# Row thresholds of a top-p attention: three guessed points for ScalarE's sums over two turns, a fourth score buffer, keys and adjacency in half the room

## The chip, the cores and the metric

The kernel runs on 1 of the 8 cores of a Trainium2 chip. The metric is the time of one execution on the device in microseconds, lower is better. PE is TensorE (matmuls and transposes), PEld its weight loads, DVE VectorE, ACT ScalarE, POOL GpSimd, SP the engine that issues the DMAs.

## The reference

Four graph layers on x (3327 x 256, padded to 26 tiles of 128 rows) with one adjacency matrix, each on relu(layernorm(x)) and added to x. The third one matters here:

```python
        logits = Q @ W2 @ K.T / TAU
        idx = jnp.argsort(-logits, axis=1)
        vals = jnp.take_along_axis(logits, idx, axis=1)
        csum = jnp.cumsum(jax.nn.softmax(vals, axis=1), axis=1)
        k_i = jnp.sum(csum < P_NUC, axis=1) + 1
        ...
        masked = jnp.where(keep, logits, -jnp.inf)
        return jax.nn.softmax(masked, axis=1)
    ...
    for s in range(STEPS):
        A = _adj_from_feats(Xa, W1, W2, W3)
        Xf = Rf @ Xf
        Xb = Rb @ Xb
        Xa = A @ Xa
        Z = Z + (Xf @ U1[s] + Xb @ U2[s] + Xa @ U3[s])
```

Q and K are Xa @ W1 and Xa @ W3, P_NUC is 0.9, STEPS is 2. So in each of two steps every row of 3327 scores needs its own threshold: the largest scores whose exponentials sum to 0.9 of the row are kept.

## The kernel before

The program is one `build()` with barriers between stages: the front (layer 0, sums of rows and columns), layer 1, the attention layer, layer 3. The change acts in the attention layer, which is software-pipelined over *turns*: `for i in range(rounds)` is unrolled on every engine, and tile t (0 to 25 are step 1, 26 to 51 step 2) passes through one stage a turn:

- turn t: `scores` on PE in four quarters k = 0 to 3 (two matmuls each on the halves of `K2` and `qt`), each quarter copied by ACT from `lg` to `E[:, t % 3]` (L1066). `neighbours` (L920) multiplies a quarter of an adjacency row block `adj` in each k, for the two linear branches.
- turn t + 1 (`exp_at`): DVE's row maximum (L1307), ACT's Exp with the sum Z (L1070) and six sums over the row, `fixed` (L1022): for each of three fixed points c the excess above c (Relu) and the count above c (Sign), two at each of k = 0, 1, 2. POOL's `bracket` (L1175 to L1219) then picks the two neighbouring points that enclose 0.9 Z.
- turn t + 2 (`search_at`): DVE's `find` (L1310). It waits for `bracketed`, makes EVALS = 3 passes in step 1 and 5 in step 2, each with `point` a trial threshold: L1345 sums the e above it, the small instructions around it (L1336 to L1349) move the ends and interpolate the next point. L1355 leaves in `U` what lies below the upper end. Then a loop takes the remaining values eight at a time in descending order (MAX8 L1368, MATCH_REPLACE L1378), one *round* or more until every one of the 128 rows has reached its share. L1394 writes the kept values back to E.
- turn t + 3 (`turn_at`): PE transposes E (L893), ACT copies to `PT` (L1062), PE multiplies with the values `Hc` (L880).
- turn t + 4 (`post_at`): scaling, dense products, and in step 2 two layer norms, whose scalars POOL computes (L1227 to L1235, L1258 to L1266).

PSUM holds one `lg` and one `tr`: a quarter's matmuls wait until ACT has copied the quarter before. ACT, DVE and POOL run their instructions in program order. In a turn ACT's order is, for each k, the PT copy, the score copy, at k = 0 the Exp and two sums, at k = 1 and 2 the copies of the dense products and two sums each, at k = 3 only copies. POOL's order is the second layer norm, the adds of Z and Y, the first layer norm, the adds of step 1, and last `bracket`. DVE's is the row maximum, then `find`.

SP loads each adjacency block in four chunks `adj[:, AGG[k]:AGG[k+1]]`; the chunk of the next block is issued as soon as `agg_part` says that this one has been used, a whole turn ahead. The stores of a turn stand behind its loads. Between the steps (`LAG` = 4 turns) nothing is scored, because step 2's keys are all of step 1's outputs; the linear branches start step 2 at `LATE` = 5.

Of the kernel before, what the change touches and what calls it, by code (L numbers as in the profile page):

```python
# [7 lines left out]
I32 = mybir.dt.int32  # L24
# [4 lines left out]
P = 128  # L29
# [4 lines left out]
EVALS = (3, 5)  # L34
MAX_AFTER = (1, 2)
AIM = 3.0
KEEP_END = 0.8

FIXED = (0.008, 0.03, 0.1)
NF = len(FIXED)  # L40
MARKED = -1.0
# [6 lines left out]
LAG = 4  # L48
LATE = 5
FIRST = 7  # L50
POINT, GAP, GOAL, MASS, BELOW = 0, 2, 3, 4, 5
# [27 lines left out]


def between_floats(value):


    t = np.float32(3 * value)
    while True:
        t = np.nextafter(t, np.float32(np.inf))
        near = [np.float32(t / np.float32(3))]
        for _ in range(2):
            near = [np.nextafter(near[0], np.float32(0))] + near + [np.nextafter(near[-1], np.float32(np.inf))]
        if all(np.float32(3) * e != t and 3 * float(e) != float(t) for e in near):  # L90
            return float(min(e for e in near if 3 * float(e) > float(t))), float(t)


def build(nc, n_nodes, xin, adjT, W0T, b0, W1g, A1T, A2, A3, UA, UB, UC, gamma, beta, tin, Wg3, out):
# [13 lines left out]
    with ctx:  # L108
# [43 lines left out]
        E = sb("E", [P, 3, NP])  # L152
# [6 lines left out]
        K2 = sb("K2", [P, NP])  # L159
# [93 lines left out]
        def layer(name, src_t, rhs, evac, dst_t, bufs):  # L253
# [6 lines left out]
            with phase_semaphores(nc, name + "_") as s:  # L260
# [11 lines left out]
                with nc.Block() as block:  # L272
# [106 lines left out]
                    def _(dve):  # L379
                        def body(u, par, live):  # L380
# [5 lines left out]
                            if live[2] and attention:  # L386
                                dve.wait_ge(dense_done, u - 1)
                                if later(u, 4):
                                    dve.wait_ge(q_out[par], 8 * (u - 2) + (0 if par == 0 else -8))
                                nc.vector.tensor_copy(K2[:, bass.ds((u - 2) * P, P)], dense[:, 0:P])  # L390
                                nc.vector.tensor_copy(qt[:, par], dense[:, P:2 * P]).then_inc(dense_copied, 1)
# [8 lines left out]
                        pipeline(dve, NT, body)  # L400

        xz = sb("xz", [P, 2, D])
# [250 lines left out]
        with ExitStack() as att:  # L653
            ab = lambda name, shape, dt=F32: att.enter_context(nc.sbuf_tensor(name, shape, dt))
            U = ab("U", [P, NPAD])
            PT = [ab(f"PT{k}", [P, 2, max(WIDE[k::2]) * P]) for k in range(2)]
# [3 lines left out]
            nmax = ab("nmax", [P, 2])  # L660
            Zs = ab("Zs", [P, 2])
            rz = ab("rz", [P, 4])
            over = ab("over", [P, 2, NF])
            sign = ab("sign", [P, 2, NF])
            neg_c = ab("neg_c", [P, NF])
            neg_3c = ab("neg_3c", [P, NF])
            half_c = ab("half_c", [P, NF])
            half_nc = ab("half_nc", [P, NF])
            table = ab("table", [P, NF + 2, 3])
            ft = ab("ft", [P, 2, NF])  # L670
            met = ab("met", [P, NF + 2])
            pick = ab("pick", [P, NF + 1])
            both = ab("both", [P, 2, NF + 1, 3])
            share = ab("share", [P, 5])
            ends2 = ab("ends2", [P, 2, 2, 3])
            trial2 = ab("trial2", [P, 2, 6])
            sp_ = ab("sp_", [P, 8])
            side = ab("side", [P, 2, 3], I32)
# [23 lines left out]
            side_at = lambda i: i - (NT + LAG + FIRST + 6) if 0 <= i - (NT + LAG + FIRST + 6) < NT // 2 else None  # L702
# [16 lines left out]
            rounds = NT + LAG + NT + 6  # L719
            early = NT - LAG  # L720
            spread = [b for i in range(rounds + 1) for b in [last_at(i)] if b is not None and i <= tiles + LATE]
# [5 lines left out]
            with phase_semaphores(nc, "att_") as s:  # L727
# [29 lines left out]
                search, rnd, fixed_done, consts = s("search_step"), s("round_step"), s("fixed_done"), s("consts")  # L757
                init, bracketed = s("bracket_step"), s("bracketed")

                with nc.Block() as block:  # L760
                    @block.sync
                    def _(sp):
                        def load_chunk(n, k):
                            j0, j1 = AGG[k], AGG[k + 1]
                            sp.dma_start(adj[:, j0:j1], adjT[n % NT, :, j0:j1]).then_inc(adj_in[k], 16)
# [5 lines left out]
                        for k in range(SLOTS):  # L771
                            load_chunk(0, k)
                        load_q(0)
                        load_q(1)
                        for i in range(rounds):
                            L, X, n = score_at(i), post_at(i), agg_at(i)
                            G = sent_at(i)
                            ahead = score_at(i + 1)
                            if ahead is not None and ahead >= 2 and ahead != NT and ahead != NT + 1:
                                sp.wait_ge(lg_done, SLOTS * (ahead - 1))  # L780
                                load_q(ahead)
                            if second(n):
                                b, q = n - NT, n % 2
                                if n >= NT + 2:
                                    sp.wait_ge(y1_done, b - 1)
                                sp.wait_ge(zg_out[b % 2], 16 * (b // 2 + 1))
                                sp.dma_start(zin[q][:, 0], zg_d[b]).then_inc(zin_in[q], 16)
                                sp.wait_ge(xo_out[b % 2], 16 * (b // 2 + 1))
                                sp.dma_start(zin[q][:, 1], xo_d[b, :, 0:D]).then_inc(zin_in[q], 16)
# [651 lines left out]
```

## Time and profile before

| | us |
|---|---|
| median of 3 runs (lowest, highest) | 3640.17 (3638.29, 3642.70) |
| span of the profiled execution | 3639.0 |
| PE busy | 3175.4 (87%) |
| DVE busy | 2635.1 (72%) |
| ACT busy | 1889.6 (52%) |
| POOL busy | 996.2 (27%) |
| PE weight loads | 2289.6 (63%) |

Busy time is the union of an engine's instructions. PE's is modelled at the ends of pipelined matmuls, so a busy PE is not a PE at its peak, and the reported lengths of POOL's instructions are rough. The first rows further down cut the attention layer at the starts of row maxima: 822 is tile 0's, 1763 tile 25's, 1871 tile 26's and 3266 tile 51's; the search of tile 51 ends at 3376, and layer 3 takes the rest. In all rows an instruction is named by its line in the kernel, its engine, its operation and `out<-in` by the program's names; a number in brackets behind an arrow is the idle time before it and what ended it.

### The profile page before, as it was taken

To read this page: it belongs to the slowest core of one execution; us is meant where nothing else is said; L and a number is where in the kernel's file an instruction comes from. 1 tells how busy PE (TensorE), PEld (TensorE's weight loads), DVE (VectorE), ACT (ScalarE), POOL (GpSimd) and SP (SyncE) were. 2 spreads that over 40 slices of the span, in tenths; PEclk is the share of its full clock that TensorE was granted. 3 is DMA by queue.
4 is the path that set the end of the run, shared out by engine and by line. 5 is a ranking of instruction groups with operands and counts; after the bars stand their busy time and mean duration, and the time that the engine had idled before them with its cause. 6 is when DMAs were issued, how large, how long until landed. Compare 5 with 4: busy or idle time off the path is not lost. (4 is left out here: it accounts for less than half of the span.)

```text
span 3639.0 us, 40362 instructions
## 1 busy us (share of the span) xinstructions
PE 3175.4 (87%) x13212; PEld 2289.6 (63%) x13212; DVE 2635.1 (72%) x3794; ACT 1889.6 (52%) x2355; POOL 996.2 (27%) x2293
## 2 busy tenths in 40 slices
PE   4999899987999999999875878667899889996799
PEld 3788688875677776777633445344555555554688
DVE  6963400006999999999839999999999999998100
ACT  2211311218788787888744556545565556563100
POOL 1212411211122221212211334334434334334211
PEclk9999999988999999999987989888999999998899
DMA  6544444432122221212221111111122222222255
GB/s 251 209 156 137 129 154 162 160 119 64 51 67 61 55 69 56 67 56 56 58 82 39 51 48 44 45 40 49 51 80 63 68 78 58 76 81 75 69 196 179
DMA packets 142416, 328.49 MB, mean 90 GB/s; under 512 B 15457, under 2 KB 95393, under 8 KB 130977
## 3 DMA queue, kind: packets, MB, share of 16 engines
q1 hardware_dynamic: 142240, 326.31, 28.3%
q8 instruction: 90, 1.47, 0.2%
q14 instruction: 86, 0.70, 0.1%
HBM read 287.59 MB, written 38.67 MB: 90 GB/s over the span
## 5 line engine op out<-in xcount | busy, mean ns | idle before, releaser
L1345 DVE SCALAR_TENSOR_TENSOR U<-E,trial 128x3327 f32<-128x3327 f32 x208 | 778.0, 3740 | 0.0
L880 PE MATMUL bank<-Hc,PT 128*128 128x256 f32 x2704 | 647.0, 392 | 68.8 <-ACT PT L1062 68.8
L880 PEld LDWEIGHTS bank<-Hc,PT 128*128 128x128 f32 x2704 | 528.0, 197 | 194.4 <-ACT PT L1062 92.3
L920 PE MATMUL bank<-big,adj 128*128 128x512 f32 x1352 | 613.7, 605 | 0.0
L1022 ACT ACTIVATE junk<-E,neg_3c 128x3327 uint8<-128x3327 f32 x156 | 479.1, 3071 | 5.1
L1022 ACT ACTIVATE junk<-E,neg_c 128x3327 uint8<-128x3327 f32 x156 | 479.6, 3074 | 1.7
L920 PEld LDWEIGHTS bank<-big,adj 128*128 128x128 f32 x1352 | 254.9, 194 | 329.4 <-issue 327.6
L893 PE MATMUL tr<-ident,E 128*128 128x128 f32 x1352 | 200.3, 291 | 275.5 <-DVE E L1394 275.5
L1062 ACT ACTIVATE PT<-tr 128x1024 f32<-128x1024 f32 x208 | 176.9, 851 | 369.2 <-PE tr L893 369.2
L893 PEld LDWEIGHTS tr<-ident,E 128*128 128x128 f32 x1352 | 172.8, 151 | 305.9 <-DVE E L1394 287.4
L920 PE MATMUL bank<-Hc,adj 128*128 128x256 f32 x1352 | 319.1, 388 | 0.0
L1368 DVE MAX8 top<-U 128x8 f32<-128x3327 f32 x81 | 293.8, 3627 | 24.5 <-DVE U L1378 12.4
L920 PEld LDWEIGHTS bank<-Hc,adj 128*128 128x128 f32 x1352 | 257.3, 194 | 82.1 <-issue 50.7
L1378 DVE MATCH_REPLACE8 U<-mark,U 128x3336 f32<-128x3336 f32 x81 | 293.1, 3618 | 0.0
L1307 DVE TENSOR_REDUCE nmax<-E 128x1 f32<-128x3327 f32 x52 | 187.8, 3611 | 109.5 <-ACT E L1066 73.8
L313 PE MATMUL bank<-big,adj 128*128 128x256 f32 x1170 | 263.6, 386 | 4.0 <-PEq L64 3.8
L313 PE MATMUL bank<-big,E 128*128 128x256 f32 x1170 | 256.8, 379 | 0.0
L313 PEld LDWEIGHTS bank<-big,adj 128*128 128x128 f32 x1170 | 224.2, 193 | 39.4 <-issue 8.8
L908 PE MATMUL lg<-K,qt 64*128 64x384 f32 (+1 forms) x832 | 223.1, 615 | 23.0 <-ACT E L1066 12.7
L313 PEld LDWEIGHTS bank<-big,E 128*128 128x128 f32 x1170 | 221.2, 190 | 29.8 <-DMA E<-adjT 0.2
L385 DVE TENSOR_TENSOR t<-bank,big 128x256 f32<-128x256 f32 x26 | 11.0, 425 | 288.3 <-PE bank L313 288.3
L1066 ACT ACTIVATE E<-lg 128x1024 f32<-128x1024 f32 x208 | 178.1, 856 | 55.1 <-PE lg L908 53.4
(231 smaller groups left out, 4481.7 us busy)
## 6 DMA issues: line engine op xcount, KB each, us to landing
adj<-adjT SPq DMA_DIRECT2D x131, 448.0 KB, 3.4
E<-adjT SPq DMA_DIRECT2D x32, 1664.0 KB, 7.0
adj<-adjT SPq DMA_DIRECT2D x104, 384.0 KB, 3.4
adj<-adjT SPq DMA_DIRECT2D x20, 1664.0 KB, 7.0
adj<-adjT SPq DMA_DIRECT2D x14, 1216.0 KB, 5.7
E<-adjT SPq DMA_DIRECT2D x13, 1216.0 KB, 5.8
xt<-xin SPq DMA_DIRECT2D x52, 128.0 KB, 5.8
x_d<-xn SPq DMA_DIRECT2D x52, 128.0 KB, 1.7
```

Source lines behind the costliest of these rows:

```text
L313: last = nc.tensor.matmul(acc[par][:, 0:D], bufs[par][:, j], rhs[:, j], start=(j == j0), stop=(j == NT - 1))
L880: last = mm(axp[:, 0:D], PT[k % 2][:, h, i * P:(i + 1) * P], Hc[:, j], start=(k == 0 and h == 0 and i == 0), stop=(k == SLOTS - 1 and h == ...
L893: last = nc.tensor.transpose(tr[:, h, i * P:(i + 1) * P], E[:, t % 3, c0:c0 + P], ident[:])
L908: last = mm(lg[:, h, 0:w], qt[rows, t % 2], K2[rows, c0:c0 + w], start=True, stop=True)
L920: last = mm(agg[:, 0:w], adj[:, j], rhs[:, j], start=(j == 0), stop=False)
L1022: go(junk[:, 0:N], E[:, t % 3, 0:N], func, bias=less[:, c:c + 1], scale=scale, accum_out=acc_[:, t % 2, c:c + 1]).then_inc(fixed_done, 1)
L1062: go(PT[k % 2][:, :, 0:w], tr[:, :, 0:w], ACT.Copy).then_inc(pt_copied, 1)
L1066: go(halves(E[:, L % 3])[:, :, c0:c0 + w], lg[:, :, 0:w], ACT.Copy).then_inc(lg_copied, 1)
L1307: V_.tensor_reduce(nmax[:, t % 2:t % 2 + 1], E[:, t % 3, 0:N], axis=AX_X, op=ALU.max, negate=True).then_inc(max_ready, 1)
L1345: V_.scalar_tensor_tensor(out=U[:, 0:N], in0=e, scalar=point, in1=e, op0=ALU.is_ge, op1=ALU.mult, accum_out=found))
L1368: rthen(V_.memset(U[:, N:NPAD], 0.0), V_.max(top8[:], U[:, 0:N]))
L1378: V_.match_replace(U[:], mark[:], U[:], MARKED).then_inc(rnd, 1)
```

## The change

- The three fixed points become three guessed ones per row. POOL's `guess(t)` computes the first from the row's mean (which the score copies now accumulate in `musum`), its maximum and Z, as if scores were normally distributed; `update(t, j)` takes ACT's sums at point j, tightens the ends and computes the next point by a Newton step with a corrected slope. ACT makes two sums at points 0 and 1 and one at point 2 (`PASSES`), five instead of six, and each now waits (`aimed[j]`) until POOL has offered the point.
- These are spread over two turns: guess, sums at point 0 and update 0 in turn t + 1; sums at points 1 and 2, updates 1 and 2 in turn t + 2 (`aim_at`); the search moves to t + 3, the transposes to t + 4, the rest to t + 5. `E` has four buffers (`DEPTH`), LAG is 5 and LATE 7, and there are two more turns in all.
- DVE's EVALS falls from (3, 5) to (2, 3). The last pass over E accumulates what it leaves, and the mass above is Z less that.
- To make room: `K2` holds keys in half the columns (each half of the partitions its own half of the keys), `adj` is used in 14 blocks and not 26, in two places of 7 (`SPAN`), so that chunk k + 2 is issued when chunk k has been used; `xz` and one `PT` lie in the rest of `adj`. SP's order in a turn changes: the stores of the last turn come behind the first chunk.
- DVE's part of layer 1 is unrolled.

```diff
-EVALS = (3, 5)
+EVALS = (2, 3)
+PASSES = (2, 2, 1)
-LAG = 4
-LATE = 5
+DEPTH = 4
+LAG = 5
+LATE = 7
+SPAN = 7
...
-            search_at = lambda i: shown(i - 2)
-            turn_at = lambda i: shown(i - 3)
-            post_at = lambda i: shown(i - 4)
+            aim_at = lambda i: shown(i - 2)
+            search_at = lambda i: shown(i - 3)
+            turn_at = lambda i: shown(i - 4)
+            post_at = lambda i: shown(i - 5)
...
+                        def sums(t, j, m):
+                            if m == 0:
+                                act.wait_ge(aimed[j], t + 1)
+                                if j > 0:
+                                    act.wait_ge(summed[j - 1], PASSES[j - 1] * (t + 1))
+                                elif t >= 1:
+                                    act.wait_ge(summed[2], t)
+                            else:
+                                act.wait_ge(summed[j], 2 * t + 1)
+                            func, acc_ = ((ACT.Relu, over), (ACT.Sign, sign))[m if j < 2 else 1]
+                            go(junk[:, 0:N], E[:, t % DEPTH, 0:N], func, bias=negp[:, t % 2, j:j + 1], scale=1.0,
+                               accum_out=acc_[:, t % 2, j:j + 1]).then_inc(summed[j], 1)
...
-                                    fixed(F, 0, 2)
+                                if k == 0 and R is not None:
+                                    sums(R, 1, 0)
+                                if k == 3 and F is not None:
+                                    sums(F, 0, 1)
-                                    if F is not None:
-                                        fixed(F, 2, 4)
+                                    if R is not None:
+                                        sums(R, 1, 1)
+                                    if R is not None:
+                                        sums(R, 2, 0)
                                     if F is not None:
-                                        fixed(F, 4, 2 * NF)
+                                        sums(F, 0, 0)
...
+                        def offer(t, j):
+                            then(ts(negp[:, t % 2, j:j + 1], cand[:, t % 2, 0:1], -UNDER, None, ALU.mult))
+                            pool.sem_inc(aimed[j], 1)
...
+                            pool.wait_ge(exp_done, t + 1)
+                            if t >= DEPTH:
+                                pool.wait_ge(probs_ready, t - DEPTH + 1)
+                            then(tt(ga[:, q, 0:2], musum[:, q, 0:2], musum[:, q, 2:4], ALU.add),
+                                 tt(ga_(2), z, root, ALU.pow))
+                            then(tt(ga_(3), ga_(0), ga_(1), ALU.add),
+                                 ts(ga_(4), ga_(2), ROOT, -ROOT - math.log(N), ALU.mult, ALU.add))
+                            then(ts(ga_(5), ga_(3), 1.0 / N, nm, ALU.mult, ALU.add))
+                            then(tt(ga_(6), ga_(4), ga_(5), ALU.subtract))
...
+                            if j > 0:
+                                then(tt(up_(16), mass_, up_(7 + j), ALU.subtract))
+                                then(ts(up_(17), up_(16), up_(16), up_(3), ALU.mult, ALU.add),
+                                     tt(up_(18), up_(16), up_(20), ALU.mult))
+                                then(tt(up_(19), up_(17), minus, ALU.pow),
+                                     tt(up_(18), up_(4), up_(18), ALU.subtract))
+                                then(tt(slope, up_(18), up_(19), ALU.mult))
...
+                                guess(F)
...
+                                update(R, 1)
...
+                                update(R, 2)
+                            if F is not None:
+                                update(F, 0)
...
-                                                         op0=ALU.is_ge, op1=ALU.subtract, reverse1=True))
+                                                         op0=ALU.is_lt, op1=ALU.mult, accum_out=sc[:, 5:6]))
+                            then(V_.tensor_tensor(mass[:, 0:1], Zs[:, q:q + 1], sc[:, 5:6], ALU.subtract))
```

`then(...)` gives each of its instructions a semaphore increment and waits for all of them before the next call. In order, with (n) instructions: guess() has the groups 2, 2, 1, 1, 2, 2, 1, 1, 1, then the offer 1, then 4, 3 and the three of `prepare`; update 0 has 14 instructions besides its `prepare`, update 1 has 21, update 2 has 22 and no `prepare`. POOL's order in a turn is: adds of Z (step 2), adds of Y, one small one, guess(F), one small one, update(R, 1), the rest of both layer norms, adds of step 1, update(R, 2), update(F, 0), and last the two adds that end step 2's tile.

## Rows read from the trace of the kernel before

**Rows 1.** By stretch: us; busy PE, PEld, DVE, ACT, POOL (instructions); PE clock; DMA share; GB/s.

```profile
822.00:1763.00 941.00, 894.20 (x4098) 668.17 (x4097) 845.66 (x1197) 779.60 (x758) 212.57 (x605) 0.97 0.21 60
1763.00:1871.00 108.00, 74.57 (x332) 55.08 (x330) 64.24 (x96) 44.84 (x55) 14.34 (x46) 0.86 0.17 52
1871.00:3266.00 1395.00, 1164.48 (x4000) 682.32 (x4001) 1299.31 (x1994) 814.60 (x899) 492.54 (x927) 0.92 0.20 59
3266.00:3376.00 110.00, 65.28 (x253) 45.25 (x252) 97.27 (x155) 39.12 (x55) 44.35 (x81) 0.84 0.26 85
```

**Rows 2.** The same view, two turns, then twelve turns of step 2.

```profile
1461.00:1498.00 37.00, 37.00 (x176) 28.08 (x175) 33.72 (x49) 31.59 (x31) 9.41 (x26) 1.00 0.22 62
2122.00:2178.00 56.00, 45.93 (x154) 26.20 (x154) 53.88 (x84) 33.35 (x38) 21.48 (x40) 0.90 0.17 49
...
2603.00:3266.00 663.00, 608.43 (x2184) 373.44 (x2183) 624.59 (x965) 404.38 (x468) 252.42 (x482) 0.96 0.24 70
```

**Rows 3.** Waits: engine and line, who it waited for, us in total, times, longest.

```profile
PE tr L893 <- DVE E L1394: 275.5, 28, 37.0
...
DVE sc L1343 <- POOLq L1218: 73.1, 29, 5.7
```

**Rows 4.** Timeline of DVE, a tile of step 1, step 2's first maximum: start, us, instruction.

```profile
1197.16 3.61 DVE L1307 TENSOR_REDUCE nmax<-E 128x1 f32<-128x3327 f32 x1
...
1200.88 3.67 DVE L1345 SCALAR_TENSOR_TENSOR U<-E,trial 128x3327 f32<-128x3327 f32 x1
...
1206.15 3.68 DVE L1345 SCALAR_TENSOR_TENSOR U<-E,trial 128x3327 f32<-128x3327 f32 x1
...
1215.71 3.68 DVE L1355 SCALAR_TENSOR_TENSOR U<-E,ends 128x3327 f32<-128x3327 f32 x1
...
1219.63 3.63 DVE L1368 MAX8 top<-U 128x8 f32<-128x3327 f32 x1 [0.24 <-DVE U L1355]
...
1228.46 3.60 DVE L1394 SCALAR_TENSOR_TENSOR E<-U,E 128x3327 f32<-128x3327 f32 x1
...
1871.28 3.62 DVE L1307 TENSOR_REDUCE nmax<-E 128x1 f32<-128x3327 f32 x1 [35.70 <-issue]
```

**Rows 5.** Timeline of DVE and POOL around one bracket, step 1.

```profile
1531.50 3.62 DVE L1394 SCALAR_TENSOR_TENSOR E<-U,E 128x3327 f32<-128x3327 f32 x1
...
1531.61 3.56 POOL L1194 TENSOR_TENSOR trial<-Zs,share 128x1 f32<-128x1 f32 x1
...
1535.96 0.19 POOL L1199 TENSOR_TENSOR trial<-trial,share 128x1 f32<-128x1 f32 x1
1536.12 0.31 POOL L1200 TENSOR_SCALAR met<-table,trial 128x3 f32<-128x3 f32 x1
1536.51 0.47 POOL L1202 TENSOR_TENSOR met<-met 128x1 f32<-128x1 f32 x2
...
1539.06 0.57 POOL L1214 TENSOR_TENSOR sp_<-sp_,share 128x1 f32<-128x1 f32 x1
1539.60 0.19 POOL L1215 TENSOR_TENSOR sp_<-sp_,ends 128x1 f32<-128x1 f32 x1
1539.87 0.20 POOL L1216 TENSOR_TENSOR sp_<-sp_ 128x1 f32<-128x1 f32 x1
```

**Rows 6.** One line of POOL (second layer norm): min/median/max ns.

```profile
L1235 POOL TENSOR_TENSOR stat<-stat x26: 191/3396/3405, 2085.2 to 3410.4; 128x1 f32<-128x1 f32 x26
```

**Rows 7.** Timeline of ACT in step 1: two sums and a fourth score copy.

```profile
1471.10 3.07 ACT L1022 ACTIVATE junk<-E,neg_c 128x3327 uint8<-128x3327 f32 x1
...
1474.30 3.07 ACT L1022 ACTIVATE junk<-E,neg_3c 128x3327 uint8<-128x3327 f32 x1
...
1495.28 0.80 ACT L1066 ACTIVATE E<-lg 128x768 f32<-128x768 f32 x1
```

**Rows 8.** DMA issues: tile, count, KB each, us to landing.

```profile
adj<-adjT SPq DMA_DIRECT2D x131, 448.0 KB, 3.4
```

**Rows 9.** Groups of DVE's instructions, stretch of step 2.

```profile
L1368 DVE MAX8 top<-U 128x8 f32<-128x3327 f32 x51 | 185.0, 3627 | 16.9 <-DVE U L1378 10.8 <-DVE U L1355 5.8 <-issue 0.3
```

More of the change, by code:

```diff
@@ L78, in pipeline @@
         static(u)
[L81 to L91, printed above, removed]
 def build(nc, n_nodes, xin, adjT, W0T, b0, W1g, A1T, A2, A3, UA, UB, UC, gamma, beta, tin, Wg3, out):
@@ L659, in build @@
             stat3 = ab("stat3", [P, 2, 8])
-            nmax = ab("nmax", [P, 2])
-            Zs = ab("Zs", [P, 2])
+            nmax = ab("nmax", [P, DEPTH])
+            Zs = ab("Zs", [P, DEPTH])
             rz = ab("rz", [P, 4])
[L663 to L678, printed above, removed]
+            musum = ab("musum", [P, 2, SLOTS])
+            over = ab("over", [P, 2, 2])
+            sign = ab("sign", [P, 2, POINTS])
+            negp = ab("negp", [P, 2, POINTS])
+            known = ab("known", [P, 8])
+            outset = ab("outset", [P, 2, 2, 2])
+            ga = ab("ga", [P, 2, 20])
+            up = ab("up", [P, 2, 24])
+            cand = ab("cand", [P, 2, 3])
+            took = ab("took", [P, 3])
+            parts = ab("parts", [P, 2, 2, 2])
+            ends2 = ab("ends2", [P, DEPTH, 2, 2])
+            trial2 = ab("trial2", [P, DEPTH, 5])
+            side = ab("side", [P, 2, 2], I32)
             sc = ab("sc", [P, 8])
@@ L718, in build @@
             last_at = lambda i: post_at(i - 2) - NT if second(post_at(i - 2)) else None
-            rounds = NT + LAG + NT + 6
+            rounds = NT + LAG + NT + 7
             early = NT - LAG
-            spread = [b for i in range(rounds + 1) for b in [last_at(i)] if b is not None and i <= tiles + LATE]
+            spread = [b for i in range(rounds + 1) for b in [last_at(i)] if b is not None and i < tiles + LATE]
             kept = len(spread)
@@ L919, in neighbours @@
                             for j in range(AGG[k], AGG[k + 1]):
-                                last = mm(agg[:, 0:w], adj[:, j], rhs[:, j], start=(j == 0), stop=False)
+                                last = mm(agg[:, 0:w], adj[:, SPAN * (k % 2) + j - AGG[k]], rhs[:, j], start=(j == 0), stop=False)
                             if k == SLOTS - 1:
@@ new lines, in _, with then, restart @@
+                        pool.wait_ge(step_done, len(values))
+                        pool.sem_clear(step_done)
+                        root, minus, half, e_ = (known[:, i:i + 1] for i in range(4))
+                        n = [0]
+                        def then(*ins):
+                            for i in ins:
+                                i.then_inc(step_done, 1)
+                            n[0] += len(ins)
+                            pool.wait_ge(step_done, n[0])
+                        def restart():
+                            pool.sem_clear(step_done)
+                            n[0] = 0
@@ L1267, in _ @@
+                            if R is not None:
+                                update(R, 2)
+                            if F is not None:
+                                update(F, 0)
+                            if second(X):
+                                b, q = X - NT, X % 2
                                 pool.wait_ge(c_ready, b + 1)
```

427 lines of the change are left out of this document (229 added, 198 removed).

## The prediction, made before the changed kernel was run

> **What bounds the kernel now.** I read the busy times by stretch first, then two short stretches inside the attention stage, then the waits, then single turns in order of time. The busy shares of the whole span say little. Cut at the first and last row maximum of each attention step [rows 1], the span falls into step 1 (941 us, tiles 0 to 25), a drain between the steps (108), step 2 (1395, tiles 26 to 51) and the last search (110); layer 3 and the front stay as they are. One turn of step 1 takes 37 us and PE is busy in all of it, while DVE has 33.7 and ACT 31.6 [rows 2] (first line). In step 2 a turn takes 56, DVE is busy 53.9 of it and PE 45.9 [rows 2] (second line). PE's longest wait is for DVE's final E, 275.5 us in 28 waits, and DVE waits 73 us for POOL's bracket [rows 3]. So step 1 is bound by PE except where a tile needs a second extraction round, step 2 by DVE. POOL is never late today: it works 213 us in step 1 and 493 in step 2 [rows 1].
>
> **What the change takes from DVE and ACT.** One pass over E with its small steps is 1206.15 - 1200.88 = 5.27 us [rows 4]. EVALS goes from (3, 5) to (2, 3): 26 x 1 + 26 x 2 = 78 passes, 411 us off DVE. A turn of DVE in step 1 falls from 33.7 to 28.4, one of step 2 by 10.5: the 53.9 are a tile with two rounds of MAX8 and MATCH_REPLACE, a round is 8.8 from 1219.63 to 1228.46 [rows 4] and 8.2 of it busy, so with one round 45.7 now and 35.2 then. ACT makes 5 sums a tile and not 6, 3.2 us each [rows 7]: 166 us off it, less 0.2 x 4 x 52 = 42 for the new row sums of the copies. The accumulated marking pass is the same pass of 3.68 us with one small step more. Moved to a turn of their own, sums and bracket are ready before DVE asks, so its 73 us of waiting go as well. If nothing else were late next, PE would be.
>
> **What it adds to POOL.** Counted from the diff, a tile now has, instead of bracket()'s 23 instructions, 87: 45 TENSOR_SCALAR, 33 TENSOR_TENSOR, 9 powers, nearly all in a chain in which each waits for the one before. Prices from POOL's bracket [rows 5]: a dependent step costs its duration and 0.08, so 0.27 for a TENSOR_TENSOR (1539.60 to 1539.87), 0.39 for a TENSOR_SCALAR (1536.12 to 1536.51), 0.65 for a power (0.57 + 0.08); all but the last of a group cost 0.16 (1535.96 to 1536.12), 0.27 and 0.54 (1539.06 to 1539.60). That gives 5.3 us for guess() up to its offer and 8.4 in all, 4.5 and 5.5 for update 0, 6.8 and 7.8 for update 1, 7.0 for update 2: 28.7 us a tile, where the bracket took 5.5. The durations alone (45 x 0.31 + 33 x 0.19 + 9 x 0.57) would be 25.3; the Trainium skill (Perfetto Trace Analysis, GPSIMD Instruction) says to time POOL by the spacing of starts and not by reported spans, which is what the steps above do; by the spans a turn would be about 3 us shorter. The TENSOR_SCALARs of the change have two operations where the one in the trace has one: bounds 0.27 (a TENSOR_TENSOR's price) and 0.51 (0.39 and 0.12 again). I take 0.39, the row of the same instruction.
>
> **What holds POOL.** A POOL instruction of 0.19 us took 3.56 at 1531.61, and ended with the pass that DVE had begun at 1531.50 [rows 5]; L1235, 128x1, has a median of 3.40 over 26, against a minimum of 0.19 [rows 6]. The first began while L1394 ran, the others while L1345 did: DVE's long passes with two inputs, E and E or U and E. While a row maximum runs, from 1535, the same kind takes 0.19 [rows 5]. So POOL stands still during each SCALAR_TENSOR_TENSOR over 3327 columns. There are 4 such passes a tile in step 1 after the change (two trials, mark, final; 14.7 us) and 5 in step 2 (18.4). The Trainium skill (SBUF — State Buffer, Who interferes with whom) has this as a lock: a DVE instruction with two SBUF inputs and a GpSimd instruction that reads SBUF exclude each other, and a reduction never takes part. It speaks against this change, the trace agrees (3.40 and 3.56 against 0.19), and where it would have the earlier one delay the other too, that falls on DVE, which gets slack.
>
> **The turn, walked through.** ACT executes in order, and its sums now wait for POOL: sums(R, 2, 0) and sums(F, 0, 0) stand at k = 2, ahead of the fourth PT copy and the fourth score copy, which let DVE's next maximum start. A sum is 3.2 us (1471.10 to 1474.30), the copy 0.8 (1495.28) [rows 7]; today no sum waits. POOL in the new turn, from the fourth copy: it waits for the last sum (3.2), then update 0 (5.5), guess (8.4), update 1 to its offer (6.8); then ACT: two sums (6.4) and two copies with the read (1.7). 32.0 us of chain. With POOL free it fits inside PE's 36.9. DVE's next maximum begins with that copy, and its passes fall at 3.7 to 7.4, 9.0 to 12.7, 13.3 to 17.0 and 26.0 to 29.6 after it ([rows 4], with one pass of 5.27 taken out). POOL has work in each of them: update 0 from 3.2 to 19.8, guess to 31.8, the offer at 38.6, sums to 45.0, copies to 46.7. 32.0 + 14.7 = 46.7 us a turn, against 941 / 25 = 37.6 now. In step 2 POOL also has the two layer norms, three adds of Z, two of Y and two at the end: some 6.0 us of it in the chain (0.8 a 256-wide one). 38.0 + 18.4 = 56.4 us, against 1395 / 25 = 55.8 now; DVE with one to three rounds (35 to 52) and PE (608 of 663 us over 12 turns, 50.7 each, third line of [rows 2]) hide in that.
>
> **The rest.** The keys in half the room: the same matmuls, and copies of half the partitions. The adjacency blocks have half a turn of lead instead of one, some 18 us for a transfer of 3.4 [rows 8]; if that cover went, a chunk would cost up to 3.4 us, four times a turn. SP issues the stores of the last turn behind the first chunk of this one: SP waits there for POOL's x3 and ACT's copies, and behind it stand the chunks for k = 3 and the next turn; they have two quarters of slack, so nothing. LAG and the fourth buffer add one turn to each drain. Between the steps, from tile 25's maximum: tile 24's update 2 ends at 49 and its search runs to 75; update 0 of tile 25 falls between its passes (offer at 65), two sums 71, update 1 behind the final pass 82, sum 85, update 2 at 92, search of 26 us to 118. Now that search ends 108 less DVE's wait of 35.7 [rows 4] after the maximum, at 72: +46. At the end, with the norms on POOL and a pass more, tile 51's update 2 comes near 114 and its search ends at 150, against 110 [rows 1]: +40. In exchange the first turns of either step, without searches, run at 20 and 35 us.
>
> **Sum,** on the profiled execution's 3639 (the median is 3640.2, 1 above; I add it): step 1: 22 + 35 + 23 x 46.7 = 1131 against 941, +190. Drain +46. Step 2: 20 + 35 + 2 x 52.8 + 55.9 + 20 x 56.4 = 1344 against 1395, -50. End +40. 3639 + 226 + 1 = 3866. Each us of chain is worth 46 us of time.
>
> **Rivals.** (a) POOL's steps are cheaper: TENSOR_SCALAR at 0.27 takes 33 x 0.12 = 4.0 us off the chain, -184; and an instruction that is already reading when a pass starts goes on beside it, some 0.2 x 4 a turn, -37: 3645, with a spread to either side of no change. Chance 0.17. (b) The other side: POOL isn't in the way, because the passes fall where it waits for ACT anyway. It decides at 36.9 - 32.0 = 4.9 us of blocked time a turn, little over one pass of the four. Then PE sets both steps: 22 + 30 + 23 x 36.9 = 901 (-40), drain +10, step 2: 20 + 30 + 10 x 45.9 + 13 x 50.7 = 1168 (-227), end +8: 3391 with the 1 above. For it: POOL works only 493 of 1395 us now [rows 1], and a turn apart there is room; against it: each of its chains is longer than DVE's gaps of 1.6 us. Chance 0.15 for anything from 3390 to 3570. (c) The change doesn't do what it says: three guesses and two or three passes leave rows further off than a bracket and three or five, and rounds multiply. Step 2 has 51 for its 26 tiles today [rows 9]. DVE passes 56.4 only from (56.4 - 35.2) / 8.2 + 1 = 3.6 rounds a tile; 4.5 would be +190: 4050. Chance 0.07. (d) TENSOR_SCALAR at 0.51: +4.0, +184: 4050; part of the forecast's upper end.
>
> **Chances.** The forecast 0.61, (a) 0.17, (b) 0.15, (c) 0.07. Range 3540 to 4010: it takes in (a), the part of (b) in which a pass or two still lie in the way, and the forecast with a TENSOR_SCALAR up to 0.47; it leaves most of (b), (c) and (d)'s end. A measurement here can tell 0.2%, 7 us. Faster: (b) and under half of (a), 0.22; same 0.04; slower 0.74.
>
> **What would show it.** In the changed kernel: POOL busy near 80% or more of the attention stage, with median durations near 3 us in a share of its 128x1 instructions; ACT's largest waits for POOL's negp; PE idle some 10 us a turn in step 1; DVE waiting for E's fourth copy, not for POOL; turns of 46.7 and 56.4 that no longer follow the number of rounds. Turns of 37 in step 1, and PE waiting for nothing, would show (b); MAX8 well over 81, (c); waits of PE on adj, the halved room.

## The result and the profile after

The changed kernel takes 3737.1 us (median of 4 executions, 3736.5 to 3738.1) against 3640.9 for the kernel before, measured beside it: 1.026 times as long, interval 1.025 to 1.028, so +96 us where +226 was forecast. The profiled execution's span is 3736.2 us, with VectorE (DVE) busy 58% of it, PE 87% and GpSimd (POOL) 64%.

By the starts of row maxima, as for the kernel before, the span falls into:

| stretch | before | forecast | after | difference | forecast difference |
|---|---|---|---|---|---|
| to tile 0's maximum | 821.8 | | 817.0 | -5 | 0 |
| step 1 (25 turns) | 941.5 | 1131 | 1081.7 | +140 | +190 |
| drain between the steps | 107.9 | 154 | 150.9 | +43 | +46 |
| step 2 (25 turns) | 1394.6 | 1344 | 1273.1 | -122 | -50 |
| tile 51's search | 109.8 | 150 | 149.5 | +40 | +40 |
| the rest | 263.3 | | 264.1 | +1 | 0 |

The same stretches, the third line of them step 2, then one turn of each step (columns as in [rows 1]: length, busy PE, PEld, DVE, ACT, POOL with instructions, PE clock, DMA share, GB/s):

```profile
817.00:1898.00 1081.00, 925.94 (x4009) 679.86 (x4008) 693.04 (x886) 692.39 (x790) 884.45 (x2154) 0.92 0.18 52
1898.00:2049.00 151.00, 98.99 (x420) 74.31 (x419) 79.00 (x109) 60.89 (x77) 68.37 (x161) 0.82 0.12 36
2049.00:3322.00 1273.00, 1122.47 (x3841) 659.88 (x3842) 960.41 (x1338) 715.96 (x918) 1079.49 (x2457) 0.94 0.21 62
3322.00:3472.00 150.00, 110.99 (x410) 74.39 (x408) 107.38 (x156) 58.13 (x86) 112.63 (x217) 0.89 0.28 87
1046.70:1091.70 45.00, 38.59 (x174) 28.57 (x173) 28.66 (x37) 28.78 (x34) 37.18 (x90) 0.96 0.19 52
2750.00:2803.70 53.70, 51.47 (x192) 31.23 (x189) 34.65 (x50) 30.23 (x41) 46.33 (x105) 1.00 0.26 72
```

Against [rows 1], DVE's load in step 1 fell from 846 to 693 us and in step 2 from 1299 to 960, as the removed passes should make it; POOL's rose from 213 to 884 and from 493 to 1079. POOL is busy 82 to 85% of both steps and the short gaps between its dependent instructions fill nearly all the rest. The largest waits say the same (engine and line, whom it waited for, us in total, times, longest):

```profile
DVE nmax L1375 <- ACT E L1070: 690.2, 46, 36.4
...
ACT junk L1027 <- POOLq L1197: 329.0, 54, 17.6
...
PE bank L882 <- ACT PT L1066: 278.2, 75, 9.5
...
POOL up L1253 <- ACT junk L1027: 61.0, 50, 6.2
PE tr L895 <- DVE E L1460: 50.3, 4, 22.4
...
DVE sc L1411 <- POOLq L1288: 75.9, 8, 20.7
```

DVE waits for the fourth score copy, ACT's sums (L1027) wait for POOL's offer of a point (L1196, L1197), PE waits for ACT's copies to `PT` that stand behind those sums; the wait of PE for DVE's final E, 275.5 in [rows 3], has shrunk to 50.3. At the head of update 0 POOL waits for ACT only 61 us in 50 turns. DVE's wait for POOL, 73 us before [rows 3], is 75.9 now, but in another place: four waits of 15 to 21 us in the two drains make up 70.7 of it, the turns only 5. It is the chain of the forecast.

One turn of step 1, from maximum to maximum: DVE's long instructions, then those of POOL that open a part of its walk or are long, then ACT's (start, us, instruction):

```profile
1046.69 3.62 DVE L1375 TENSOR_REDUCE nmax<-E 128x1 f32<-128x3327 f32 x1 [15.41 <-ACT E L1070]
1050.42 3.68 DVE L1413 SCALAR_TENSOR_TENSOR U<-E,trial 128x3327 f32<-128x3327 f32 x1
1055.69 3.68 DVE L1413 SCALAR_TENSOR_TENSOR U<-E,trial 128x3327 f32<-128x3327 f32 x1
1059.89 3.68 DVE L1420 SCALAR_TENSOR_TENSOR U<-E,ends 128x3327 f32<-128x3327 f32 x1
...
1068.79 3.62 DVE L1444 MATCH_REPLACE8 U<-mark,U 128x3336 f32<-128x3336 f32 x1
...
1072.69 3.61 DVE L1460 SCALAR_TENSOR_TENSOR E<-U,E 128x3327 f32<-128x3327 f32 x1
1091.72 3.62 DVE L1375 TENSOR_REDUCE nmax<-E 128x1 f32<-128x3327 f32 x1 [15.42 <-ACT E L1070]
```

```profile
1049.72 0.19 POOL L1253 TENSOR_SCALAR up<-sign 128x1 f32<-128x1 f32 x1 [1.31 <-ACT junk L1027]
...
1050.46 3.81 POOL L1261 TENSOR_SCALAR cand<-up 128x2 f32<-128x2 f32 x1
...
1055.64 0.57 POOL L1277 TENSOR_TENSOR up<-known,up 128x1 f32<-128x1 f32 x1
1056.19 3.24 POOL L1278 TENSOR_TENSOR ends<-parts 128x4 f32<-128x4 f32 x1
...
1059.82 3.79 POOL L1283 TENSOR_SCALAR cand<-up,ends 128x1 f32<-128x1 f32 x1
...
1065.37 0.19 POOL L1216 TENSOR_TENSOR ga<-musum 128x2 f32<-128x2 f32 x1 [0.24 <-POOL up L1204]
...
1069.36 0.55 POOL L1228 TENSOR_TENSOR cand<-known,ga 128x1 f32<-128x1 f32 x1
...
1071.03 0.57 POOL L1234 TENSOR_TENSOR ga<-Zs,known 128x1 f32<-128x1 f32 x1
...
1072.65 3.78 POOL L1202 TENSOR_SCALAR up<-known,cand,ga 128x2 f32<-128x2 f32 x1
...
1077.26 0.19 POOL L1253 TENSOR_SCALAR up<-sign 128x1 f32<-128x1 f32 x1 [0.19 <-POOL up L1204]
...
1083.42 0.21 POOL L1196 TENSOR_SCALAR negp<-cand 128x1 f32<-128x1 f32 x1
```

```profile
1083.72 3.07 ACT L1027 ACTIVATE junk<-E,negp 128x3327 uint8<-128x3327 f32 x1 [5.37 <-POOLq L1197]
1086.97 3.07 ACT L1027 ACTIVATE junk<-E,negp 128x3327 uint8<-128x3327 f32 x1
1090.04 0.79 ACT L1066 ACTIVATE PT<-tr 128x768 f32<-128x768 f32 x1
1090.73 0.80 ACT L1070 ACTIVATE E<-lg 128x768 f32<-128x768 f32 x1
```

Read it as the forecast walked it. POOL waits for the last sum until 1049.72 (L1253 opens update 0), the guess begins at 1065.37 (L1216), update 1 at 1077.26, its offer at 1083.42 starts ACT's two sums at 1083.72, the two copies follow, and the next maximum stands at 1091.72: 45.03 us. Four POOL instructions of 3.2 to 3.8 us lie in it, each ending within 0.2 us of the end of one of the four two-input passes.

### The profile page after: what moved, and what is told of

The parts are those of the page before. It is cut to its first block and busy times, and to the rows that moved or that the text cites. A ratio compares the mean times of both kernels' runs of the same rounds, so it can differ in the third digit from the quotient of the medians.

```text
span 3736.2 us, 43278 instructions
## 1 busy us (share of the span) xinstructions
PE 3234.8 (87%) x13212; PEld 2326.9 (62%) x13212; DVE 2169.4 (58%) x2838; ACT 1739.3 (47%) x2461; POOL 2374.9 (64%) x5618
## 5 line engine op out<-in xcount | busy, mean ns | idle before, releaser
L1027 ACT ACTIVATE junk<-E,negp 128x3327 uint8<-128x3327 f32 x260 | 797.6, 3068 | 548.9 <-POOLq L1197 329.0
L882 PE MATMUL bank<-Hc,PT 128*128 128x256 f32 x1248 | 392.6, 479 | 278.2 <-ACT PT L1066 278.2
L882 PEld LDWEIGHTS bank<-Hc,PT 128*128 128x128 f32 x1248 | 297.3, 244 | 378.5 <-ACT PT L1066 321.8
L1413 DVE SCALAR_TENSOR_TENSOR U<-E,trial 128x3327 f32<-128x3327 f32 x130 | 479.3, 3687 | 0.0
L922 PEld LDWEIGHTS bank<-big,adj 128*128 128x128 f32 x1352 | 250.9, 190 | 319.9 <-issue 318.9
L294 PE MATMUL bank<-big,E 128*128 128x256 f32 x1664 | 365.6, 381 | 4.1 <-DMA E<-adjT 2.1
L882 PE MATMUL bank<-Hc,adj 128*128 128x256 f32 x1456 | 340.2, 386 | 13.8 <-ACT adj L1066 13.8
L882 PEld LDWEIGHTS bank<-Hc,adj 128*128 128x128 f32 x1456 | 281.4, 194 | 77.4 <-issue 23.4
L922 PE MATMUL bank<-Hc,adj 128*128 128x256 f32 x1352 | 317.9, 387 | 5.5 <-ACT bias L1047 5.4
L922 PEld LDWEIGHTS bank<-Hc,adj 128*128 128x128 f32 x1352 | 256.6, 193 | 85.3 <-issue 54.0
L895 PE MATMUL tr<-ident,E 128*128 128x128 f32 x1352 | 187.9, 279 | 50.4 <-DVE E L1460 50.3
L1261 POOL TENSOR_SCALAR cand<-up 128x2 f32<-128x2 f32 x156 | 201.1, 1289 | 15.6
L1420 DVE SCALAR_TENSOR_TENSOR U<-E,ends 128x3327 f32<-128x3327 f32 x52 | 201.7, 3878 | 2.2
```

The source lines that it names most:

```text
L294: last = nc.tensor.matmul(acc[par][:, 0:D], bufs[par][:, j], rhs[:, j], start=(j == j0), stop=(j == NT - 1))
L882: last = mm(axp[:, 0:D], PT[k % 2][:, h, i * P:(i + 1) * P], Hc[:, j], start=(k == 0 and h == 0 and i == 0), stop=(k == SLOTS - 1 and h == ...
L895: last = nc.tensor.transpose(tr[:, h, i * P:(i + 1) * P], E[:, t % DEPTH, c0:c0 + P], ident[:])
L922: last = mm(agg[:, 0:w], adj[:, SPAN * (k % 2) + j - AGG[k]], rhs[:, j], start=(j == 0), stop=False)
L1027: go(junk[:, 0:N], E[:, t % DEPTH, 0:N], func, bias=negp[:, t % 2, j:j + 1], scale=1.0, accum_out=acc_[:, t % 2, j:j + 1]).then_inc(summed ...
L1261: then(ts(cand[:, q, 1:3], up[:, q, 0:2], mass_, None, ALU.add), ts(took[:, 1:2], reach, tgt, None, ALU.is_ge))
```

## Experiments

In order of what they tell, not of when they ran. Each was timed over 4 executions; the kernel before, run beside them, had medians of 3640.5 to 3641.2. The rounds named are executions of MAX8 (81 before, 75 in the changed kernel: 29 in step 1, 46 in step 2). The length of a turn is the median of the 25 turns of its step, unless one turn is named.

**One more pass of DVE a tile, with two inputs or with one.** Ahead of the trial loop a pass over E whose sum nobody uses:

```diff
                             dve.wait_ge(bracketed, t + 1)
+                            # e1
+                            then(V_.scalar_tensor_tensor(out=U[:, 0:N], in0=e, scalar=point, in1=e,
+                                                         op0=ALU.is_ge, op1=ALU.mult, accum_out=sc[:, 7:8]))
+                            # e2, in its place
+                            then(V_.tensor_reduce(sc[:, 7:8], e, axis=AX_X, op=ALU.max))
```

> The changed kernel with one more pass in each search, of the kind of its trials: two inputs, E and E, 3.68 us, into U, which the next pass overwrites. The result does not change. VectorE is idle some 16 us of a turn of 45 in step 1. Theory (POOL's chain sets the turn, and every two-input pass holds it up): a turn of step 1 goes from 45.0 to 48.7, one of step 2 from 53.8 to 57.5, the drains by 10 to 15 in all: about +185, 3920 us. Rival (the turn is the chain through POOL and ACT alone, VectorE has slack): turns stay at 45.0 and 53.8, +15 from the drains: 3750.

> The changed kernel with one more pass in each search as well, but a reduction with one input (3.6 us, a maximum over E into an unused scalar). Theory (the lock between two-input passes and POOL): turns stay at 45.0 and 53.8, only the drains grow: +10 to +20, 3750 us. Rival (it is VectorE's time as such that counts, whatever the pass reads): as the two-input pass, +170 to +190.

Measured: 3908.7 us with the two-input pass (+172 against the changed kernel; turns of 48.2 and 57.4 instead of 45.0 and 53.7), 3736.4 with the one-input pass (no change; turns 44.8 and 53.6, those of step 2 now spread from 47 to 62, step 2 as a whole again 1273). Both passes keep DVE busy for about as long (3.68 and 3.61 us). The added reduction of the second kernel runs from 1140.97 to 1144.58, and POOL works through it at full pace, twelve instructions begun; with the next two-input pass, begun at 1144.81, it stops. That kernel, DVE then POOL:

```profile
1140.97 3.61 DVE L1401 TENSOR_REDUCE sc<-E 128x1 f32<-128x3327 f32 x1
1144.81 3.68 DVE L1414 SCALAR_TENSOR_TENSOR U<-E,trial 128x3327 f32<-128x3327 f32 x1
```

```profile
1141.20 0.31 POOL L1261 TENSOR_SCALAR cand<-up 128x2 f32<-128x2 f32 x1
...
1143.68 0.19 POOL L1279 TENSOR_TENSOR up<-up,cand 128x1 f32<-128x1 f32 x1
...
1144.87 3.84 POOL L1202 TENSOR_SCALAR up<-known,cand,ga 128x2 f32<-128x2 f32 x1 [0.22 <-POOL negp L1196]
```

So it is not DVE's time that costs, it is what a two-input pass does to POOL. The two added passes differ in one more thing: the first also writes all its columns to `U`, the second a single one. The changed kernel's trace settles that. MATCH_REPLACE8 reads and writes 3336 columns, with a single input of that width, and POOL runs beside it at its usual pace (1068.79 in the turn above, with the powers of 1069.36 and 1071.03 at 0.55 and 0.57 us). In the 75 rounds no POOL instruction begun beside MAX8 or MATCH_REPLACE8 took over 0.74 us.

**One pass of trial less a tile.** `EVALS = (2, 3)` becomes `(1, 2)`.

> The changed kernel with one pass of trial less in each tile (1 and 2 in place of 2 and 3), so that more is left to the rounds of MAX8 and MATCH_REPLACE8. Theory: a pass that reads two inputs holds GpSimd for its whole length while a round does not, and GpSimd's walk bounds the turn: each turn is shorter by 3.2 to 3.7 us (45.0 to 41.6 and 53.7 to 50.2), whatever the rounds do, as long as VectorE does not become the bound; over 51 turns 3560 to 3590 us. Rival: the rounds that come in its place (7.2 us each on VectorE, perhaps 20 to 40 of them) land on the path: 3737 or more.

Measured: 3603.3 us (ratio to before 0.990, interval 0.988 to 0.991). Turns of 41.9 and 50.6, each 3.1 us shorter, while the rounds rose from 75 to 119:

```profile
L1434 DVE MAX8 top<-U 128x8 f32<-128x3327 f32 x119 | 431.6, 3627 | 41.8 <-DVE U L1444 29.5 <-DVE mass L1422 12.3
```

44 rounds more, some 8 us of DVE each, and 134 us less time: the turn follows POOL and not DVE. It falls 13 us outside what was expected; the drain grew by 7 us, and some tiles of step 1 with four rounds took turns of 51 us.

**Ten more instructions on POOL**, at the head of update 0, each waiting for the one before:

```diff
+                            if j == 0:
+                                for _ in range(10):   # e8
+                                    then(ts(padded[:], known[:, 0:1], 1.0, 0.0, ALU.mult, ALU.add))
+                            # e9, in its place: ts(padded[:], known[:, 0:1], known[:, 1:2], known[:, 2:3], ...)
                             then(ts(count, sign[:, q, j:j + 1], 0.5, N / 2, ALU.mult, ALU.add))
```

> The changed kernel with ten more TENSOR_SCALAR on GpSimd in a row, each waiting for the one before, at the head of update 0, with two constants and no scalar read from memory (their results are used nowhere). Theory: GpSimd's walk round the turn is the bound, so each of some 48 turns grows by ten steps. At the 0.27 us that the changed kernel's trace shows for such a step: +2.7 us a turn, 3860 to 3875 us. At the 0.39 us that the prediction took: +3.9 us a turn, 3920 to 3930 us. If GpSimd is not the bound of a turn: below 3780 us.

> As the run with ten more TENSOR_SCALAR on GpSimd, but each of the ten reads its two scalars from memory instead of having them as constants. The run with constants grew by 146 us, 2.8 us a turn. Theory: the price of this operation depends on how many scalars it reads; the changed kernel's trace shows 0.43 us a step for two of them, so +4.3 us a turn over 51 turns: 3737 + 220 = 3957 us, some 73 above the run with constants. If the scalars cost nothing and the difference in the trace has another reason: 3883 us again.

Measured: 3883.2 us with constants (turns 47.8 and 56.5, +2.8 each), 3979.5 with scalars from memory (49.5 and 58.6, +4.5 and +4.9). The added instructions in either kernel (min/median/max ns; the maxima are held by passes):

```profile
L1256 POOL TENSOR_SCALAR padded<-known x520: 190/191/3692, 840.7 to 3534.1; 128x1 f32<-128x1 f32 x174
```

```profile
L1256 POOL TENSOR_SCALAR padded<-known x520: 343/345/3887, 841.1 to 3634.5; 128x1 f32<-128x1 f32 x174
```

A dependent TENSOR_SCALAR costs 0.28 us with two constants and 0.45 with two scalars read from memory; [rows 5]' 0.39 for an instruction with one such scalar was taken for all 45. The second kernel came out 22 us above what was expected, the first 8 to 23. Both show that the walk of POOL is the turn, at about one us of turn for one us of walk, in both steps.

**ACT's sums of the new point before the last sum of the old one.** At k = 2 the order is turned (the semaphore waits in `sums()`, which are not shown, are fitted to it):

```diff
-                                    if R is not None:
-                                        sums(R, 2, 0)
                                     if F is not None:
                                         sums(F, 0, 0)
+                                    if R is not None:
+                                        sums(R, 2, 0)
```

> The changed kernel with ScalarE's sums(F, 0, 0) ahead of sums(R, 2, 0) at k = 2: it then fills the 6 us in which ScalarE waits for update 1. Theory A (the ring through both engines sets the turn: update 0, guess, update 1, two sums, two copies, a sum): 3.2 us off the ring, turns of 41.8 and 50.6, -147: 3590 us. Theory B (POOL's own work with the passes that hold it, 43.5 of the 45.0, is the next bound at once): 1.5 a turn, -65: 3670.

Measured: 3717.7 us, -19. Both expectations were too large. The turn of step 1 fell by 1.1 us (45.0 to 43.9), that of step 2 by 0.2. POOL sat idle 1.3 us a turn of step 1 before update 0 ([1.31 <-ACT junk L1027] in the timeline above), and 0.36 in the turn of step 2 shown further down. Nearly all of that is gone now (25.9 us in 9 waits in place of 61.0 in 50), and it was all there was: with POOL at work in the whole turn, moving ACT's sums can't shorten it. The mechanism is theory B's, at 1.1 us where it had 1.5, and in step 1 only. Theory A counted the sum as part of a chain, although POOL has another update to do meanwhile.

**Two guessed points instead of three, in both steps.** `PASSES = (2, 2)`, no update 2.

> The changed kernel with two guessed points and not three: no sums(R, 2, 0), no update 2, update 1 gives the search's first point. POOL loses 22 instructions and 7 us a turn, ScalarE a sum. Theory (POOL sets the turn): a turn of step 1 falls from 45.0 to PE's 37, one of step 2 from 53.8 to 47 to 50, if rounds stay near 29 and 46: about 3440 us. Rival (fewer points cost as much in rounds as they save): rounds above 2 a tile in step 1 and 2.7 in step 2, where VectorE takes over: 3600 to 3750.

Measured: 3752.9 us. POOL's walk is shorter by 27 instructions a turn, and step 1 still grew, from 1082 to 1171: its rounds went from 29 to 79, and DVE is busy 1067 of 1171 us. Step 2 shrank, from 1273 to 1208, with 59 rounds in place of 46, and the last search from 150 to 129. So the third point earns its time in step 1 and not in step 2, although there the rounds already come unevenly: one tile needs nine, and one turn takes 105.5 us.

**The guess taken back.** The frame of the change stays (fourth buffer, one turn more, half room); in step 1 or in both steps the fixed points, six sums and `bracket` of the kernel before come back (cut; in e5 two constants of the interpolation in step 2, `AIM` and `KEEP_END`, also get their values of before):

```diff
-EVALS = (2, 3)
+EVALS = (3, 5)                  # e5; (3, 3) in e6 and e7
+FIXED_STEP = (True, True)       # e5; (True, False) in e6 and e7
+LAST = (2, 2)                   # last guessed point; (2, 1) in e7
...
-                            if F is not None:
-                                guess(F)
+                            if isg(F):
+                                guess(F)
...
+                            if isf(F):
+                                bracket(F)
```

> The changed kernel with the guess taken back in both steps: three fixed points, six sums and the bracket of the kernel before, with 3 and 5 rounds of trial; the fourth score buffer, the longer order of turns and the half room stay. If all of the loss of step 1 is the chain of guess and update, step 1 takes 940 us again (turns 36.9), the drain between the steps about 120, and step 2 loses the wait for the bracket that the kernel before had (73 us in all): about 1330; in all 3570 to 3640 us. If the loss came from the fourth buffer or the longer order, the turns of step 1 stay at 42 us or more: 3730 or more.

> Step 1 with the three fixed points and its 3 rounds, step 2 with the three guessed points and its 3 rounds. If the two steps are bounded apart from each other, step 1 and the drain take about 150 + 25 us less than in the changed kernel and step 2 stays at 1273: 3540 to 3580 us, below the kernel before by 2 to 3%. If the guess's load in step 2 depended on the points of step 1 (it doesn't by the chain), 3650 or more.

> As the run with fixed points in step 1, but step 2 takes two guessed points instead of three. The run with two points in both steps had a step 2 of 1208 us and a last search of 129 us: so 3450 to 3500 us if the steps are independent; 3560 or more if the third point is what keeps step 2's rounds down.

Measured: 3600.4, 3554.0 and 3468.7 us. With the guess out of both steps the frame alone is worth 40 us: step 1 takes 914 and step 2 1325, and DVE's wait for the bracket, 73 us in [rows 3], is no longer among the forty largest. Which part of the frame gives how much of the 40, no run separates. Set against this kernel, the guess with its fewer passes costs 168 us in step 1 (1082 for 914) and gains 52 in step 2 (1273 for 1325): of the 122 us that step 2 gained in the change, the frame alone has 69. Fixed points in step 1 and three guessed ones in step 2 give 914 and 1273, the two halves of the other kernels put together. With two guessed points in step 2 the kernel is 4.7% faster than the kernel before (ratio 0.953, interval 0.951 to 0.954). Its step 1, drain, step 2 and last search:

```profile
818.60:1732.00 913.40, 873.61 (x3998) 650.01 (x3997) 819.91 (x1173) 783.13 (x850) 249.99 (x603) 0.98 0.22 62
1732.00:1867.00 135.00, 95.67 (x432) 72.57 (x431) 95.38 (x146) 51.92 (x70) 25.60 (x48) 0.88 0.14 41
1867.00:3075.00 1208.00, 1074.34 (x3810) 630.61 (x3811) 1073.18 (x1470) 652.50 (x872) 898.00 (x1820) 0.94 0.22 64
3075.00:3204.00 129.00, 113.41 (x441) 75.90 (x439) 114.64 (x167) 52.33 (x81) 96.63 (x151) 0.97 0.34 106
```

PE is busy 874 of 913 us in step 1, and in the last turns of step 2 nearly all the time:

```profile
2680.00:3075.00 395.00, 391.68 (x1457) 242.14 (x1456) 339.74 (x470) 224.75 (x313) 317.88 (x616) 1.00 0.27 79
```

**The same with a pass less in step 2**, `EVALS = (3, 2)`:

> The kernel with fixed points in step 1 and two guessed points in step 2, with 2 passes of trial in step 2 in place of 3. Theory: with two points GpSimd's walk is no longer what bounds step 2 (the turns take 48.7 us, TensorE's own work in a turn some 45), and the rounds are already 59; a pass less saves 3.7 us a tile on VectorE and costs 20 or more rounds of 7.2: 3450 to 3500 us, about the same as with 3 passes (3469). If the lock of the pass still bounds the turns: 3400 or less.

Measured: 3677.5 us, a miss, 209 above the kernel with three passes. The rounds of step 2 went from 59 to 104 and the median turn only from 48.7 to 49.3, but seven tiles had five rounds or more (one before), one of them eleven, and there are turns of up to 120 us. I had counted rounds as a mean that DVE's slack could hide; they come in lumps. (Rounds of the whole attention layer:)

```profile
L1536 DVE MAX8 top<-U 128x8 f32<-128x3327 f32 x134 | 486.0, 3627 | 43.6 <-DVE U L1546 32.0 <-DVE mass L1524 11.5
```

## Why the prediction was right or wrong

**What the change takes from DVE and ACT** was right: over the whole execution DVE has 466 us less to do (411 were charged for the removed passes, and six rounds fewer are some 50 more) and ACT 150 (124 forecast), and PE hardly waits for DVE any more. The 153 and 339 us by which DVE's load fell in the two steps overstate it a little, because with the later search a part of it has moved to the drains.

**What holds POOL** was right as a mechanism, shown by the pair of added passes, and a little too dear. Each pass was charged its whole 3.68 us. In the turn above the four held instructions cost 3.81, 3.24, 3.79 and 3.78 in place of the 0.30, 0.20, 0.33 and 0.34 that they take undisturbed: 13.45 in all, 3.4 a pass, against 14.7. It is no single turn's number: over the last 22 turns of step 1 four instructions a turn were held, for 13.5 us beyond their shortest time, and over the last 21 of step 2 five, for 16.6. The rows before the change had this already: 3.56 less 0.19 is 3.37 [rows 5], and the median of 3.40 less 0.19 is 3.2 [rows 6]. The prediction read these lines as a halt during each pass and then charged the pass's own 3.68. What POOL has begun when a pass starts is finished first: the L1278 held for 3.24 waited behind a power of 0.57 (L1277) that had begun 0.05 before the pass of 1055.69. A pass added costs 3.2 and 3.7 us a turn, one removed saves 3.1. The Trainium skill (SBUF — State Buffer, Who interferes with whom) has the pair locked for a whole instruction and lets the order of issue decide who waits; the rows agree where POOL came second, with its instructions at 3.2 to 3.8 us. Where POOL came first they agree only in part: the power of 1055.64 left the pass of 1055.69 at 3.68 us (more in the last section).

**The chain of a turn** was right in all its links. Measured on the turn above, with the held time taken out, against the forecast: wait for the last sum 3.0 (3.2), update 0 with its offer and the preparation 5.6 (5.5), guess 8.5 (8.4), update 1 to its offer 6.5 (6.8), two sums 6.3 (6.4), copies 1.7 (1.7). 31.6 against 32.0. The price of 0.39 for every TENSOR_SCALAR was wrong one by one (0.28 to 0.45), but the instructions of the chain have zero, one and two scalars from memory in such a mix that POOL's three links come to 20.6 against 20.7. That is luck and not a right price. The bounds of 0.27 and 0.51 held. One thing the walk didn't compare: POOL's own work in the turn, with the passes that hold it, is only 1.3 us shorter than the turn, so that the wait for the last sum is a link nearly without weight (ACT's sums turned round gave 1.1).

**The step that failed: two terms of the sum were mis-sized, the turn and the first turns.** The turn was forecast 1.7 us too long in step 1 (46.7 against 45.0) and 2.7 in step 2 (56.4 against 53.7). Of the first, 1.3 is the price of a pass, charged at 3.68 and measured at 3.4, and 0.4 the links, as above. In the step 2 turn from 2750 to 2803.7, five POOL instructions were held:

```profile
2750.26 3.99 POOL L1361 TENSOR_TENSOR kq<-xo,cc 128x256 f32<-128x256 f32 x1
...
2763.35 3.50 POOL L1231 TENSOR_TENSOR parts<-Zs,outset 128x4 f32<-128x4 f32 x1 [0.18 <-POOL negp L1196]
...
2788.45 3.82 POOL L1261 TENSOR_SCALAR cand<-up 128x2 f32<-128x2 f32 x1
2794.19 3.24 POOL L1278 TENSOR_TENSOR ends<-parts 128x4 f32<-128x4 f32 x1
2799.13 3.69 POOL L1203 TENSOR_SCALAR up<-cand 128x1 f32<-128x1 f32 x1
2803.18 0.72 POOL L1354 TENSOR_TENSOR cc<-cc,gam 128x256 f32<-128x256 f32 x1
```

Their excess over 0.73, 0.20, 0.30, 0.20 and 0.26 is 16.5 us (18.4 charged), and the rest of the turn 37.2 (38.0). The error of a turn is multiplied by some 46 turns, as the prediction itself said: the last 22 turns of step 1 are 40 us less than forecast, the last 21 of step 2 55. The first turns of either step came 25 us shorter in all. In step 1 they were put at 22, 35 and 46.7 and came at 19.9, 30.8 and 44.1; in step 2 at 20, 35, 52.8 and 52.8, and came at 15.7, 30.8, 53.5 and 44.7. The first two of either step, which have no search and so no passes, are 15 of the 25; the prediction gives no working for them. With 3 from the drain and 4 from the stretches outside, that is all but 2 of the 129 between 3866 and 3737. The error is 4 to 5% of each turn. But the gain and the loss of the change nearly cancel, and so this error of 129 us is more than the whole measured difference of 96.

**Drain and end**, walked link by link, came out at +43 and +40 against +46 and +40. Between the steps the links are there one by one: the searches of tiles 24 and 25 began 47 and 88.5 us after tile 25's maximum (49 and 92 forecast), and the last one ended at 115 (118). That the end fits to the us is luck: tile 51's update 2 was done 106 us after its maximum, where some 114 was forecast, and its search, with two rounds, took 44 us and not 36.

**Rivals.** (a) had a cheaper TENSOR_SCALAR and 0.2 us off each pass, and put the time at 3645: its two reasons are both there in part, its size isn't (1.7 and 2.7 us off a turn, where it had 4.8). (b), POOL not in the way, fell in both steps: ten instructions more lengthen the turn by their whole length, where PE as the bound would hide them. Its point of decision (4.9 us of blocked time a turn) was passed with 13.5. (c), rounds multiplying, did not happen with three points (75 for 81), but did with two in step 1 (79 for 29) and with a pass less (119 for 75).

**Signs.** POOL at 82 and 85% of the two steps, ACT waiting for the offers, DVE for the fourth copy, and turns that don't follow the rounds (tiles of step 2 with one to three rounds all take 53.4 to 54.0) came as written. PE's idle was forecast at 10 us a turn and is 6.4 of 45.0.

## What to carry to other kernels

Before small scalar work goes to GpSimd, lay its chain beside VectorE's passes: each long pass with two inputs stops it for nearly that pass, while a reduction, MAX8 or MATCH_REPLACE8 doesn't, so a pass saved on VectorE can be worth more to GpSimd than to VectorE. Ask of each stage alone whether a moved computation pays: here the same guess, against the frame without it, lost 168 us in the step bound by TensorE and won 52 in the one bound by VectorE, and splitting it by stage turned a kernel 2.6% slower into one 2.4% faster (3554.0 us), and 4.7% with one point less in step 2. Where a forecast is one turn's length multiplied by some fifty turns, take what each stop costs from the rows that show it (the held length less the undisturbed one), and not from the length of the instruction that causes it: two us a turn were here as much as the whole result.

## What the runs showed of the hardware that I had not expected

- The price of a GpSimd TENSOR_SCALAR on 128x1 hangs on its scalars: 191 ns (0.28 us as a dependent step) with two constants, 345 ns (0.45) with two read from memory; L1203 and L1220, with one, take 0.26 and 0.27. As cheap as a TENSOR_TENSOR (0.19) only in the first case.
- The holding goes both ways. The marking pass of 2803.21 in step 2 took 4.17 us instead of 3.68; POOL's L1354 (128x256, 0.72 us, shown above) had begun 0.03 us before it. The power of 1055.64 in step 1 (0.57 us), begun 0.05 us before a pass, left that pass at 3.68. Over the attention layer of the changed kernel 25 of the 234 two-input passes took 4.1 to 4.2 us. Each of the 25 began within 0.1 us of the start of a POOL instruction of 128x256 (0.72 us), and none of the passes that began while POOL was at a 128x1 to 128x4 one was longer than usual, 48 of them behind a power of 0.57. So the size of POOL's instruction separates the two, though no run here says by what. DVE's last trial pass and the marking pass of that step 2 turn:

```profile
2799.01 3.68 DVE L1413 SCALAR_TENSOR_TENSOR U<-E,trial 128x3327 f32<-128x3327 f32 x1
2803.21 4.17 DVE L1420 SCALAR_TENSOR_TENSOR U<-E,ends 128x3327 f32<-128x3327 f32 x1
```

- The granted TensorE clock fell with PE's idle: 0.97 in step 1 before [rows 1], 0.92 after, 0.98 again in the kernel with fixed points in step 1. The links of the step 1 turn that add up to its 45.0 us are POOL's, ACT's and the passes', none is PE's, so no cost of the lower clock is seen in it; no run here tests that by itself.
